# Reordering the input loads, the constants' queue and the first statistics of a macaron block on one Trainium2 core

## The chip, the cores and the metric

The kernel runs on 1 core of one Trainium2 chip. The metric is the device time in microseconds (us) of one execution. A core has TensorE (PE, with its weight loads PEld), VectorE (DVE), ScalarE (ACT), GpSimd (POOL) and SyncE (SP), which only issues DMAs here. All DMAs of a core share 16 DMA engines.

## The reference, cut to what matters

Four sequences of 512 tokens with 512 features go through half a feed-forward network, a Mamba-2 mixer and half a feed-forward network again, each with a layer norm in front and a residual behind. The weights of the feed-forward network are seen through a Walsh-Hadamard transform (fwht), random signs and scales:

```python
def ffn(x):                                   # INTER = 2048, SCALE = 64
    x = fwht(x * SU_ug) / SCALE
    up   = x @ W_up.T   * (Wscale_ug[:INTER] * SCALE)
    gate = x @ W_gate.T * (Wscale_ug[INTER:] * SCALE)
    x = fwht(silu(gate) * up * SU_dp) / SCALE
    return x @ W_down.T * (Wscale_dp * SCALE)

x = x + 0.5 * ffn(layernorm(x))
x = x + mixer(layernorm(x))
x = x + 0.5 * ffn(layernorm(x))
```

The change touches only what stands ahead of and in the first pieces of the first feed-forward network.

## The kernel before

`program` lays out the memory and calls `begin` (the first feed-forward network for two sequences, and the preparation of all weights) and `mixer` (everything after). Only `begin` is changed. Each engine has its own program in it (`@block.sync`, `gpsimd`, `tensor`, `scalar`, `vector`), and runs it strictly in the order written; semaphores tie the five together.

**Transforming the weights.** The Hadamard transform is folded into the weights. The down weights `wdn` come in FB = 16 *groups* of 256 KB. A group i is loaded by SP into `group_tile(i)` (parts of `res`, `draw`, `mraw`, `last`, L346), multiplied on PE by the small Hadamard matrix `H16` (L464, bank 4 + i % 4), copied out of the bank by ACT (L588), scaled by `wdp`, and stored by SP into the HBM buffer `mid_s` ("down_half" in the trace, L367). Who scales depends on i: POOL for i < 4 (L434), VectorE straight out of the bank for even i of 8 and above (L711), and VectorE after ACT's copy for the others (L714). The later stage of the down weights reads two 128-row blocks of `mid_s` at a time (`fetch_down`, L308), and SP waits for all 16 stores before the first of them.

The up and gate weights come in NC = 8 chunks of 1 MB in `raw` (`fetch`, L300). Four elementwise operations, the *butterflies* (VectorE at L785 and L788 for chunk 0, POOL at L412 and L416 for the others), and then one *turn* for each of KH = 4 blocks transform them: a PE matmul with the Hadamard matrix H (L492), a high part rounded by ACT (L600) and a low part made by VectorE (L726), both into `wu`. `keep_up` stores `wu` to HBM (2 MB) for the later network (L312).

**x.** A tile of 128 tokens is loaded into `res` (x of sequence 0 by L351, of sequence 1 by L352, of both others by L375), VectorE takes its statistics (`bn_stats`, L792) and computes the inverse root in some 20 tiny dependent operations (`roots`, with `rsqrt`, L162 to L139), `bias` (L741) finishes it and raises `s_mv`, ACT normalizes the rows (`rows`, L614), PE transposes them (`turn(("x", c, t))`, four 128 x 128 transposes, L484), ACT makes the high part (L596) and VectorE the low part (L722). The roots of both sequences are computed together, for 8 tiles at once.

**Order.** PE does groups 0 to 3, the 4 turns of chunk 0 ("ug", 0, k), groups 4 to 7, the 4 turns of sequence 0 ("x", 0, t), groups 8 and 9. Then *units* follow, n = 0 to 15: unit n is chunk n // 2 of the weights for sequence n % 2. A unit has four `up(n, j)` of 12 matmuls (L508), and between them what `unit_turns(n)` says; in unit 0 also groups 10 to 15. `turns` numbers the turns in order of execution; the number picks the PSUM bank (`turn_bank`: `U[i % 4]` for the first eight, then two banks `T`), and for i of 10 and above PE waits for the low part of turn i - 2 (`s_tl`). At the end of unit 1 stands `down(0)`, and the first turn of the down weights ("dn", 0, 0) (L495) is in unit 1 behind `up(1, 1)`; it needs `fetch_down(0)`.

SP's queue before: the four constant loads (`cs` twice, `pr`, `wdp`, all on `s_par`), `fetch(0)`, groups 0 to 3, x of sequence 0, x of sequence 1, then a wait for x of sequence 0 to have landed (`s_x0`), groups 4 to 11, `fetch(1)`, groups 12 to 15, the scales `sc`, and then the 16 stores in order, with `fetch(2)` behind the store of group 4 and `keep_up(0)` behind that of group 8.

Of the kernel before, what the change touches and what calls it, by code (L numbers as in the profile page):

```python
# [57 lines left out]
def run(steps):  # L58
    for _ in steps:
        pass  # L60
# [110 lines left out]
def begin(nc, s, x, wug, wsc, wdn, win, wout, cst, par, ug_s, dn_s, in_s, out_s, mid_s):  # L171
# [6 lines left out]
    turns = {}  # L178
    for key in ([("ug", 0, k) for k in range(KH)] + [("x", 0, t) for t in range(TPG)] + [("x", 1, t) for t in range(TPG)]
                + [("ug", 1, 0), ("dn", 0, 0), ("ug", 1, 1), ("dn", 0, 1), ("ug", 1, 2), ("ug", 1, 3)]):  # L180
        turns[key] = len(turns)
# [12 lines left out]
    with ExitStack() as ctx:  # L194
# [17 lines left out]
        st, mv = sb("st", [P, 2 * TPG, 6]), sb("mv", [P, 4, 2 * TPG])  # L212
        s_par, s_c, s_ex, s_x0, s_x1, s_x, s_sc = (sem(n) for n in "par c ex x0 x1 x sc".split())
        s_g, s_gv, s_gc, s_gp, s_gw, s_gs = (sem(n) for n in "g gv gc gp gw gs".split())
# [20 lines left out]
        def by_vector(i):  # L235

            return i >= 8 and i % 2 == 0

# [27 lines left out]
        def unit_turns(n):  # L266

            c, g = n // 2, n % 2
            if n == 0:
                return (), (("x", 1, 0), ("x", 1, 1)), (("x", 1, 2), ("x", 1, 3)), ()  # L270
            if n == 1:
                return (), (("ug", 1, 0), ("dn", 0, 0)), (("ug", 1, 1), ("dn", 0, 1)), (("ug", 1, 2), ("ug", 1, 3))
            if n == UNITS - 2:
                return (("dn", c, 0),), (("dn", c, 1),), (("x", 2, 0), ("x", 2, 1)), (("x", 2, 2), ("x", 2, 3))
            if n == UNITS - 1:
                return (), (), (), ()
            return (("dn", c, g),), (("ug", c + 1, 2 * g),), (("ug", c + 1, 2 * g + 1),), ()
# [15 lines left out]
        def _(sp):  # L293
# [46 lines left out]
            xt = x.rearrange("(t p) n -> p t n", p=P)  # L340
            sp.dma_start(cs[:, 0:C_I2], cst[:, 0:C_I2]).then_inc(s_par, 16)
            sp.dma_start(cs[:, C_I2:C_END], cst[:, 5 * P:5 * P + HEADS]).then_inc(s_par, 16)
            sp.dma_start(pr[:], par[:, 0:P_WDP]).then_inc(s_par, 16)
            sp.dma_start(wdp[:], par[:, P_WDP:P_END]).then_inc(s_par, 16)
            def load_group(i):
                sp.dma_start(group_tile(i), wdn[PQ * i:PQ * (i + 1)].rearrange("i (a n) -> a i n", a=FB)).then_inc(s_gl[i], 16)  # L346

            fetch(0)
            for i in range(4):
                load_group(i)  # L350
            sp.dma_start(res[:, 0:TPG, :], xt[:, 0:TPG, :]).then_inc(s_x0, 16)  # L351
            sp.dma_start(res[:, TPG:2 * TPG, :], xt[:, TPG:2 * TPG, :]).then_inc(s_x1, 16)  # L352
            sp.wait_ge(s_x0, 16)
            for i in range(4, 12):
                load_group(i)
            fetch(1)
            for i in range(12, FB):
                load_group(i)
            sp.dma_start(sc[:], wsc.rearrange("c p n -> p c n")).then_inc(s_sc, 16)
            for i in range(FB):  # L360
                if i < 4:
                    sp.wait_ge(s_gp, i + 1)
                elif by_vector(i):
                    sp.wait_ge(s_gv, scaled_before(i) + 1)
                else:
                    sp.wait_ge(s_gw, copies(i) - 3)
                sp.dma_start(mid_s[:, PQ * i:PQ * (i + 1), :], group_tile(i)).then_inc(s_gs, 16)  # L367
                if i == 4:
                    fetch(2)
                if i == 8:  # L370
                    keep_up(0)
            sp.wait_ge(s_gs, 16 * FB)
            fetch_down(0)
            fetch_down(1)
            sp.dma_start(res[:, 2 * TPG:NT, :], xt[:, 2 * TPG:NT, :]).then_inc(s_x, 16)  # L375
            fetch(3)
            keep_down(0)
            fetch_down(2)
            keep_up(1)
            for c in range(1, NC):  # L380
# [24 lines left out]
        def _(pool):  # L405
# [24 lines left out]

            pool.wait_ge(s_par, 64)
            for i in range(4):
                pool.wait_ge(s_gc, i + 1)
                pool.tensor_tensor(group_tile(i), group_tile(i), wdp[:], ALU.mult).then_inc(s_gp, 1)  # L434
            pool.wait_ge(s_gw, FB // 2)
            butterflies(1, False)
# [14 lines left out]
        def _(pe):  # L451
# [100 lines left out]

            pe.wait_ge(s_par, 64)
            pe.wait_ge(s_c, 8)
            for i in range(4):
                group(i)
            for k in range(KH):
                turn(("ug", 0, k))
            for i in range(4, 8):
                group(i)  # L560
            for t in range(TPG):
                turn(("x", 0, t))
            group(8)
            group(9)
            for n in range(UNITS):
# [19 lines left out]
        def _(act):  # L585
# [21 lines left out]
            def rows(c, ts=range(TPG)):  # L607

                act.wait_ge(s_mv, max(1, c))
                if c:  # L610
                    act.wait_ge(s_tm, turns["x", c - 1, TPG - 1] + 1)
                for t in ts:
                    at = TPG * (0, 1, 1, 0)[c] + t
                    act.activation(xn[:, t, :], res[:, TPG * (0, 1, 2, 0)[c] + t, :], ACT.Identity,  # L614
                                   bias=mv[:, 1, at:at + 1], scale=mv[:, 3, at:at + 1]).then_inc(s_row, 1)
# [30 lines left out]

            act.wait_ge(s_par, 64)
            act.activation(s["acol"][:], pr[:, P_ALOG:P_ALOG + 1], ACT.Exp).then_inc(s_ex, 1)
            act.wait_ge(s_c, 8)
            for i in range(4):  # L650
                group(i)
            for k in range(KH):
                turn(("ug", 0, k))
            group(4)
            group(5)
            rows(0)
            for t in range(TPG):
                turn(("x", 0, t))
            group(6)
            group(7)  # L660
            group(9)
            rows(1)
            act.wait_ge(s_sc, 16)
# [6 lines left out]
            for n in range(UNITS - 1):  # L670
                keys = unit_turns(n)
                silu(n, 0)
                if n == 0:
                    group(11)
                    group(13)
                for key in keys[0]:
                    turn(key)
                silu(n, 1)
                if n == 0:
                    group(15)  # L680
                for key in keys[1]:
                    turn(key)
                if n == UNITS - 2:
                    rows(2)
                for key in keys[2]:
                    turn(key)
                for j in range(2):
                    hidden_high(n, j)
                for key in keys[3]:
                    turn(key)  # L690
                high_blocks(n)
                for key in halves_of(n + 1):
                    high_half(key)
# [11 lines left out]
        def _(dve):  # L705
# [64 lines left out]
            dve.memset(s["ones"][:], 1.0).then_inc(s_c, 1)  # L770
            dve.wait_ge(s_par, 64)
            dve.tensor_reduce(eight[:], I.rearrange("p (a i) -> p i a", i=PQ), mybir.AxisListType.X, ALU.add).then_inc(s_c, 1)
# [8 lines left out]
            dve.wait_ge(s_ex, 1)  # L781
            dve.tensor_scalar(s["acol"][:], s["acol"][:], -1.0, None, ALU.mult).then_inc(s_c, 1)
            dve.wait_ge(s_fr[0], 16)
            for n, op in enumerate((ALU.add, ALU.subtract)):
                dve.tensor_tensor(t1[:, n::2, :], raw[:, 0, 0::2, :], raw[:, 0, 1::2, :], op).then_inc(s_b0, 1)  # L785
            dve.wait_ge(s_b0, 2)
            for n, op in enumerate((ALU.add, ALU.subtract)):
                dve.tensor_tensor(raw[:, 0, 2 * n:2 * n + 2, :], t1[:, 0:2, :], t1[:, 2:4, :], op).then_inc(s_b0, 1)  # L788
            for landed, c in ((s_x0, 0), (s_x1, 1)):
                dve.wait_ge(landed, 16)  # L790
                for t in range(TPG * c, TPG * c + TPG):
                    own.done(dve.bn_stats(st[:, t, :], res[:, t, :]))  # L792
            run(roots(dve, st, mv, own))
            bias(0, 2 * TPG)
            for k in range(KH):
                turn(("ug", 0, k))
            for t in range(TPG):
                turn(("x", 0, t))
            for i in (8, 4, 5, 6, 7, 9):
                group(i)  # L800
            def low_blocks(n):
# [6 lines left out]
            for n in range(UNITS - 1):  # L808
                keys = unit_turns(n)
                if n == 0:  # L810
                    for i in range(10, 14):
                        group(i)
                for key in keys[0]:
                    turn(key)
                if n == 0:
                    group(14)
                    group(15)
                for key in keys[1]:
                    turn(key)
                if n == 0:  # L820
                    for key in keys[2]:
                        turn(key)
                hidden(n, 0)
                if n:
                    for key in keys[2]:
                        turn(key)
                hidden(n, 1)
# [1358 lines left out]
```

## Time and profile before

| | |
|---|---|
| median of 3 runs | 1654.56 us (1654.16 to 1661.31) |
| profiled execution, its own time | 1658.09 us |
| its span | 1656.2 us |
| PE busy | 1621.9 us, 98% of the span |
| VectorE, ScalarE, GpSimd busy | 1033.3, 626.5 and 377.0 us |
| first matmul starts | 11.37 us |
| first `up` starts | 32.64 us |
| second unit's first `up` starts | 51.39 us |
| DMA in the first 60 us | 17.44 MB, 291 GB/s |

The profile is one execution; its span is 1.9 us shorter than that execution's own time. The timeline names engine, line, output and input tile, and behind an entry in brackets, how long the engine had been idle and what released it. "xN" merges N instructions of one kind. A matmul of f32 is recorded as two entries.

### The profile page before, as it was taken

What the parts mean: (1) busy time and instruction counts of PE and PEld (TensorE: products, weight loads), DVE (VectorE), ACT (ScalarE), POOL (GpSimd) and SP (SyncE); (2) the same over time, 40 slices, a digit from 0 to 9 for tenths busy, and PEclk for the clock granted to TensorE, in tenths of its full rate; (3) what the DMA queues carried; (4) which work ended last, traced back from release to release, by engine and by line L of the source; (5) the groups of instructions that cost most, each with busy time, mean ns of one, the idle gap of its engine ahead of it and who ended that gap; (6) DMA issues with size and microseconds to landing.
All of it is one profiled execution on the core that took longest, in us unless ns stands there. A gap on an engine that the chain in (4) does not pass through costs nothing.

```text
span 1656.2 us, 25046 instructions
## 1 busy us (share of the span) xinstructions
PE 1621.9 (98%) x9672; PEld 1311.9 (79%) x9672; DVE 1033.3 (62%) x2022; ACT 626.5 (38%) x934; POOL 377.0 (23%) x298
## 2 busy tenths in 40 slices
PE   6999999989999999999999999999999999999999
PEld 3788788867888778888877888877888877888887
DVE  6444345766676877777786677777675683543333
ACT  4334334454333464333355334256333341122111
POOL 1655662012222212222122122122122121000000
PEclk9999999999999999999999999999999999999999
DMA  9755654744455354444435445545544447556763
GB/s 286 293 190 208 224 196 165 254 167 157 155 157 167 130 176 148 158 161 151 163 119 174 165 150 166 162 135 184 165 155 156 155 128 217 166 178 187 219 199 131
DMA packets 253427, 290.46 MB, mean 175 GB/s; under 512 B 14464, under 2 KB 211200, under 8 KB 244096
## 3 DMA queue, kind: packets, MB, share of 16 engines
q1 hardware_dynamic: 253312, 288.88, 53.4%
q8 instruction: 78, 1.28, 0.3%
q14 instruction: 37, 0.30, 0.1%
HBM read 238.51 MB, written 50.33 MB: 174 GB/s over the span
## 4 chain that ended last, share of the span: by engine, by line
PE 72%; DVE 4%; ACT 2%; issue 1%; DMA 0%; SPq 0%; ACTq 0%; DVEq 0%
PE bank L1184 30%; PE bank L1225 14%; PE bank L1140 12%; PE bank L1253 5%; PE bank L1322 3%; PE bank L1293 2%; PE bank L1309 2%; PE bank L1271 2%; PE bank L1316 1%; PE bank L1281 1%; DVE xT L1740 0%; DVE m_cv L1781 0%; DVE res L1766 0%; PE bank L1168 0%; PE bank L1150 0%
## 5 line engine op out<-in xcount | busy, mean ns | idle before, releaser
L1184 PE MATMUL bank<-fxT,wj 128*128 128x512 f32 x1752 | 415.3, 390 | 1.2 <-DVE xn L1753 1.2
L1184 PEld LDWEIGHTS bank<-fxT,wj 128*128 128x128 f32 x1752 | 328.7, 188 | 70.1 <-DVE xn L1753 1.7
L1225 PE MATMUL bank<-m_wd,m_hb 128*128 128x512 f32 x1128 | 278.8, 393 | 1.9 <-DVE m_hb L1759 1.9
L1225 PEld LDWEIGHTS bank<-m_wd,m_hb 128*128 128x128 f32 x1128 | 209.1, 188 | 47.3 <-issue 5.0
L1535 ACT CAST m_hb<-xn 128x512 fp32r<-128x512 f32 x96 | 59.5, 620 | 455.1 <-DVE xn L1753 455.1
L1140 PE MATMUL bank<-xT,wi 128*128 128x512 f32 x900 | 222.6, 395 | 1.6 <-DVE m_cv L1781 0.5
L1140 PEld LDWEIGHTS bank<-xT,wi 128*128 128x128 f32 x900 | 166.1, 188 | 39.1 <-issue 4.5
L1766 DVE TENSOR_TENSOR res<-bank,res 128x512 f32<-128x512 f32 x192 | 132.5, 690 | 83.4 <-PE bank L1225 81.2
L2084 POOL TENSOR_TENSOR m_L<-m_L,m_GT 128x512 f32<-128x512 f32 x36 | 52.6, 1461 | 436.0 <-ACT m_L L1544 436.0
L1753 DVE SCALAR_TENSOR_TENSOR xn<-bank,sc,xn 128x512 f32<-128x512 f32 x96 | 71.8, 748 | 123.0 <-PE bank L1184 122.9
L1529 ACT ACTIVATE xn<-bank,sc 128x512 f32<-128x512 f32 x96 | 66.1, 688 | 145.8 <-PE bank L1184 140.3
L1544 ACT ACTIVATE m_L<-bank 128x512 f32<-128x512 f32 x128 | 76.5, 598 | 84.1 <-PE bank L1271 83.8
L1759 DVE TENSOR_TENSOR m_hb<-xn,m_hb 128x512 fp32r<-128x512 f32 x96 | 66.3, 691 | 56.0 <-ACT m_hb L1535 56.0
L1781 DVE SCALAR_TENSOR_TENSOR m_cv<-bank,pr,m_cv 128x511 f32<-128x511 f32 (+2 forms) x120 | 89.6, 747 | 11.4 <-ACT m_cv L1489 8.6
L508 PE MATMUL bank<-xT,b_wu 128*128 128x512 f32 x384 | 95.5, 397 | 0.0
L508 PE MATMUL bank<-b_xT,b_wu 128*128 128x512 f32 x384 | 93.0, 392 | 0.0
L1253 PE MATMUL bank<-m_wo,m_yh 128*128 128x512 f32 x384 | 90.8, 391 | 0.7 <-ACT xn L1529 0.7
L549 PE MATMUL bank<-b_wd,b_hb 128*128 128x512 f32 x384 | 90.9, 392 | 0.0
L2111 POOL TENSOR_TENSOR m_ss<-m_ss,m_y 128x512 f32<-128x512 f32 x28 | 36.2, 1293 | 239.6 <-ACT m_y L1564 239.6
L508 PEld LDWEIGHTS bank<-xT,b_wu 128*128 128x128 f32 x384 | 71.8, 188 | 17.9 <-DVE xT L722 0.5
L1253 PEld LDWEIGHTS bank<-m_wo,m_yh 128*128 128x128 f32 x384 | 71.6, 188 | 17.7 <-issue 1.9
L508 PEld LDWEIGHTS bank<-b_xT,b_wu 128*128 128x128 f32 x384 | 72.1, 188 | 16.3 <-issue 0.7
(222 smaller groups left out, 2312.4 us busy)
## 6 DMA issues: line engine op xcount, KB each, us to landing
wj<-ug_split SPq DMA_DIRECT2D x167, 512.0 KB, 4.2
m_wd<-dn_split SPq DMA_DIRECT2D x48, 1024.0 KB, 4.8
wi<-in_split SPq DMA_DIRECT2D x76, 512.0 KB, 3.3
ug_split<-b_wu SPq DMA_DIRECT2D x8, 2048.0 KB, 14.1
m_wo<-out_split SPq DMA_DIRECT2D x32, 512.0 KB, 4.1
wi<-ug_split SPq DMA_DIRECT2D x25, 512.0 KB, 4.1
in_split<-b_msp SPq DMA_DIRECT2D x20, 512.0 KB, 3.7
raw<-in_wug SPq DMA_DIRECT2D x8, 1024.0 KB, 7.0
```

The costliest lines, as they stand in the source:

```text
L508: ins = pe.matmul(U[j][:], wu[c % 2][:, a, k, ck(j)], xT[g][:, b, k, :], start=(k == 0 and i == 0), stop=(k == KH - 1 and i == 2))
L549: ins = pe.matmul(down_bank(n, t)[:], hb[:, n % 2, a, j, ck(t)], wd[c % 2][:, b, j, :], start=(j == 0 and i == 0), stop=(j == 1 and i == 2))
L1140: ins = pe.matmul(to[:], w[:, a, k, :], xT[:, b, k, :], start=(k == 0 and i == 0), stop=(k == KH - 1 and i == 2))
L1184: ins = pe.matmul(to[:], w[:, a, k, :], frm[:, b, k, :], start=(k == 0 and i == 0), stop=(k == KH - 1 and i == 2))
L1225: ins = pe.matmul(F[t % 2][:], hb[:, a, j, ck(t)], wd[:, b, j, :], start=(j == 0 and n == 0), stop=(j == 1 and n == 2))
L1253: ins = pe.matmul(F[1 - t % 2][:], yh[:, (2 * pair + i) % 4, a, ck(t)], wout[i][:, b, :], start=(i == 0 and n == 0), stop=(i == 1 and n == 2))
L1529: act.activation(hf[:, j, :], F[1][:], ACT.Silu, scale=sc[:, at % NC, j:j + 1]).then_inc(s_sil, 1)
L1544: act.activation(L[:, b % 2, j, :], A[:], ACT.Exp).then_inc(s_L, 1)
L1753: dve.scalar_tensor_tensor(hf[:, j, :], F[0][:], sc[:, at % NC, 2 + j:3 + j], hf[:, j, :], ALU.mult, ALU.mult).then_inc(s_h, 1)
L1759: dve.tensor_tensor(hb[:, 1, j, :], hf[:, j, :], hb[:, 0, j, :].bitcast(F32), ALU.subtract).then_inc(s_lo, 1)
L1766: dve.tensor_tensor(r, frm[:], r, ALU.add).then_inc(s_acc, 1)
L1781: ins = dve.scalar_tensor_tensor(cv[:, d:SEQ], frm[:, 0:SEQ - d], pr[:, w + 3 - d:w + 4 - d], cv[:, d:SEQ], ALU.mult, ALU.add)
```

## The change

- SP's queue: x of sequence 0 is the first load, then groups 0 to 3, `fetch(0)`, groups 4 to 7, x of sequence 1, groups 8 to 15, `fetch(1)`; the wait for x of sequence 0 is gone. `fetch(2)` moves to just ahead of the store of group 15, and `keep_up(0)` behind `fetch_down(1)`. A wait on `s_us` stands ahead of `keep_up(1)`.
- The constants and `sc` are issued by ScalarE. `wdp` gets a semaphore of its own, `s_wdp`, so what needs only `cs` and `pr` no longer waits for it.
- POOL scales groups 0 to 7 (before: 0 to 3), VectorE 8 to 15. The predicate `by_vector` gives the same answers as before.
- PE and ScalarE: behind groups 0 to 3 come the turns of x of sequence 0, groups 4 and 5, the turns of chunk 0, and groups 6 to 9 (ACT: 6, 7 and 9).
- VectorE: the statistics and roots of sequence 0 alone come first, ahead of the butterflies of chunk 0; those of sequence 1 are done between groups 9 and 12, in three pieces around groups 10 and 11.
- Unit 0: all four turns of sequence 1 come behind `up(0, 2)` (before: two behind `up(0, 1)`, two behind `up(0, 2)`). ACT's `rows(1)` comes behind its copy of group 15; VectorE does `hidden(0, 0)` ahead of those turns' low parts.

```diff
-    for key in ([("ug", 0, k) for k in range(KH)] + [("x", 0, t) for t in range(TPG)] + [("x", 1, t) for t in range(TPG)]
+    for key in ([("x", 0, t) for t in range(TPG)] + [("ug", 0, k) for k in range(KH)] + [("x", 1, t) for t in range(TPG)]
...
-                return (), (("x", 1, 0), ("x", 1, 1)), (("x", 1, 2), ("x", 1, 3)), ()
+                return (), (), tuple(("x", 1, t) for t in range(TPG)), ()
...
@@ SP
-            fetch(0)
+            sp.dma_start(res[:, 0:TPG, :], xt[:, 0:TPG, :]).then_inc(s_x0, 16)
             for i in range(4):
                 load_group(i)
-            sp.dma_start(res[:, 0:TPG, :], xt[:, 0:TPG, :]).then_inc(s_x0, 16)
+            fetch(0)
+            for i in range(4, 8):
+                load_group(i)
             sp.dma_start(res[:, TPG:2 * TPG, :], xt[:, TPG:2 * TPG, :]).then_inc(s_x1, 16)
-            sp.wait_ge(s_x0, 16)
-            for i in range(4, 12):
+            for i in range(8, FB):
                 load_group(i)
             fetch(1)
-            for i in range(12, FB):
-                load_group(i)
-            sp.dma_start(sc[:], wsc.rearrange("c p n -> p c n")).then_inc(s_sc, 16)
             for i in range(FB):
-                if i < 4:
+                if i == FB - 1:
+                    fetch(2)
+                if i < FB // 2:
                     sp.wait_ge(s_gp, i + 1)
...
-                    sp.wait_ge(s_gw, copies(i) - 3)
+                    sp.wait_ge(s_gw, copies(i) - FB // 2 + 1)
                 sp.dma_start(mid_s[:, PQ * i:PQ * (i + 1), :], group_tile(i)).then_inc(s_gs, 16)
-                if i == 4:
-                    fetch(2)
-                if i == 8:
-                    keep_up(0)
             sp.wait_ge(s_gs, 16 * FB)
             fetch_down(0)
             fetch_down(1)
+            keep_up(0)
...
+            sp.wait_ge(s_us, 16)
             keep_up(1)
@@ POOL
-            pool.wait_ge(s_par, 64)
-            for i in range(4):
+            pool.wait_ge(s_wdp, 16)
+            for i in range(FB // 2):
...
-            pool.wait_ge(s_gw, FB // 2)
+            pool.wait_ge(s_gw, FB // 4)
@@ PE
-            pe.wait_ge(s_par, 64)
+            pe.wait_ge(s_par, 48)
...
+            for t in range(TPG):
+                turn(("x", 0, t))
+            group(4)
+            group(5)
             for k in range(KH):
                 turn(("ug", 0, k))
-            for i in range(4, 8):
+            for i in range(6, 10):
                 group(i)
-            for t in range(TPG):
-                turn(("x", 0, t))
-            group(8)
-            group(9)
@@ ACT
+            act.dma_start(cs[:, 0:C_I2], cst[:, 0:C_I2]).then_inc(s_par, 16)
+            act.dma_start(pr[:], par[:, 0:P_WDP]).then_inc(s_par, 16)
+            act.dma_start(cs[:, C_I2:C_END], cst[:, 5 * P:5 * P + HEADS]).then_inc(s_par, 16)
+            act.dma_start(wdp[:], par[:, P_WDP:P_END]).then_inc(s_wdp, 16)
+            act.dma_start(sc[:], wsc.rearrange("c p n -> p c n")).then_inc(s_sc, 16)
+            act.wait_ge(s_par, 48)
...
-            for k in range(KH):
-                turn(("ug", 0, k))
-            group(4)
-            group(5)
             rows(0)
             for t in range(TPG):
                 turn(("x", 0, t))
+            group(4)
+            group(5)
+            for k in range(KH):
+                turn(("ug", 0, k))
             group(6)
             group(7)
             group(9)
-            rows(1)
...
                 if n == 0:
                     group(15)
+                    rows(1)
@@ VectorE
+            dve.wait_ge(s_x0, 16)
+            for t in range(TPG):
+                own.done(dve.bn_stats(st[:, t, :], res[:, t, :]))
+            run(roots(dve, st[:, 0:TPG], mv[:, :, 0:TPG], own))
+            bias(0, TPG)
             dve.wait_ge(s_fr[0], 16)
...
-            for landed, c in ((s_x0, 0), (s_x1, 1)):
-                dve.wait_ge(landed, 16)
-                for t in range(TPG * c, TPG * c + TPG):
-                    own.done(dve.bn_stats(st[:, t, :], res[:, t, :]))
-            run(roots(dve, st, mv, own))
-            bias(0, 2 * TPG)
+            for t in range(TPG):
+                turn(("x", 0, t))
             for k in range(KH):
                 turn(("ug", 0, k))
-            for t in range(TPG):
-                turn(("x", 0, t))
-            for i in (8, 4, 5, 6, 7, 9):
-                group(i)
+            dve.wait_ge(s_wdp, 16)
+            group(8)
+            group(9)
+            second = stats(TPG, TPG, TPG)
+            dve.wait_ge(s_x1, 16)
+            next(second)
+            next(second)
+            group(10)
+            group(11)
+            next(second)
+            bias(TPG, TPG)
```

## Rows read from the trace of the kernel before

**Rows 1.** Busy time by stage: stretch, its us, each engine, granted clock, DMA share, GB/s.

```profile
0.00:11.37 11.37, 0.00 (x1) 0.04 (x1) 2.32 (x9) 1.49 (x2) 0.20 (x4) 1.00 0.82 232
11.37:32.64 21.27, 17.64 (x44) 8.55 (x44) 17.46 (x44) 12.09 (x20) 5.72 (x4) 0.92 0.98 286
32.64:60.00 27.36, 25.90 (x106) 18.23 (x105) 15.57 (x21) 13.18 (x21) 14.63 (x6) 1.00 0.88 318
60.00:470.00 410.00, 401.24 (x2089) 325.16 (x2088) 226.10 (x409) 168.87 (x266) 154.27 (x109) 1.00 0.56 194
...
27.60:31.10 3.50, 3.47 (x17) 3.33 (x18) 2.67 (x5) 3.43 (x6) 0.00 (x0) 0.53 1.01 327
```

**Rows 2.** PE's timeline, 11 to 57 us.

```profile
11.37 5.07 PE L464 MATMUL bank<-res,b_H 128*128 128x512 f32 x8 [11.37 <-DMA res<-in_wdn]
16.27 3.60 PE L492 MATMUL bank<-raw,cs 128*128 128x512 f32 x8
20.83 4.13 PE L464 MATMUL bank<-res,b_H 128*128 128x512 f32 x8 [0.97 <-DMA res<-in_wdn]
27.63 3.50 PE L484 MATMUL bank<-cs,xn 128*128 128x128 f32 x16 [2.67 <-ACT xn L614]
30.92 2.04 PE L464 MATMUL bank<-draw,b_H 128*128 128x512 f32 x4
32.64 3.13 PE L508 MATMUL bank<-xT,b_wu 128*128 128x512 f32 x12
...
44.01 1.09 PE L484 MATMUL bank<-cs,xn 128*128 128x128 f32 x8 [0.29 <-DVE last L711]
...
51.39 5.66 PE L508 MATMUL bank<-b_xT,b_wu 128*128 128x512 f32 x24
```

**Rows 3.** Durations (ns min/median/max) of the matmuls of the first groups.

```profile
L464 PE MATMUL bank<-res,b_H x8: 592/625/1192, 11.4 to 15.8; 128*128 128x512 f32 x8
```

**Rows 4.** ScalarE's timeline, 13 to 30 us.

```profile
13.51 0.59 ACT L588 COPY res<-bank 128x512 f32<-128x512 f32 x1 [8.32 <-PE bank L464]
...
26.67 2.93 ACT L614 ACTIVATE xn<-res,b_mv 128x512 f32<-128x512 f32 x4 [3.09 <-DVE b_mv L741]
```

**Rows 5.** VectorE's timeline, 4 to 33 us.

```profile
4.99 0.38 DVE L772 TENSOR_REDUCE b_eight<-cs 128x8 f32<-128x128 f32 x1 [3.99 <-DMA b_wdp<-in_par]
...
12.79 2.36 DVE L788 TENSOR_TENSOR raw<-b_t 128x1024 f32<-128x1024 f32 x2
16.65 2.47 DVE L792 BATCH_NORM_STATS2 b_st<-res 128x6 f32<-128x512 f32 x4 [1.50 <-DMA res<-in_x]
19.88 2.48 DVE L792 BATCH_NORM_STATS2 b_st<-res 128x6 f32<-128x512 f32 x4 [0.76 <-DMA res<-in_x]
...
26.47 0.17 DVE L741 SCALAR_TENSOR_TENSOR b_mv<-b_mv 128x8 f32<-128x8 f32 x1
...
30.10 2.49 DVE L722 TENSOR_TENSOR xT<-bank,xT 128x512 fp32r<-128x512 f32 x4 [0.83 <-ACT xT L596]
```

**Rows 6.** POOL's timeline, 14 to 56 us.

```profile
14.24 5.72 POOL L434 TENSOR_TENSOR res<-res,b_wdp 128x512 f32<-128x512 f32 x4 [13.80 <-ACT res L588]
45.15 4.74 POOL L412 TENSOR_TENSOR b_t<-raw 128x1024 f32<-128x1024 f32 x2 [25.19 <-DVE last L714]
49.97 5.29 POOL L416 TENSOR_TENSOR raw<-b_t 128x1024 f32<-128x1024 f32 x2
```

**Rows 7.** Durations, as in rows 3, of POOL's scaling and of VectorE's low parts.

```profile
L434 POOL TENSOR_TENSOR res<-res,b_wdp x4: 1262/1266/2034, 14.2 to 18.7; 128x512 f32<-128x512 f32 x4
...
L753 DVE TENSOR_TENSOR b_hb<-b_hf,b_hb x32: 679/687/2715, 52.3 to 329.3; 128x512 fp32r<-128x512 f32 x32
```

**Rows 8.** DMA issues, 0 to 60 us: count, KB each, median us to landing.

```profile
draw<-down_half SPq DMA_DIRECT2D x2, 512.0 KB, 4.1
...
down_half<-last SPq DMA_DIRECT2D x2, 256.0 KB, 6.2
```

**Rows 9.** What PE waited for, 0 to 62 us: total, times, longest.

```profile
PE bank L495 <- DMA draw<-down_half: 1.2, 1, 1.2
```

More of the change, by code:

```diff
@@ L212, in begin @@
         st, mv = sb("st", [P, 2 * TPG, 6]), sb("mv", [P, 4, 2 * TPG])
-        s_par, s_c, s_ex, s_x0, s_x1, s_x, s_sc = (sem(n) for n in "par c ex x0 x1 x sc".split())
+        s_par, s_wdp, s_c, s_ex, s_x0, s_x1, s_x, s_sc = (sem(n) for n in "par wdp c ex x0 x1 x sc".split())
         s_g, s_gv, s_gc, s_gp, s_gw, s_gs = (sem(n) for n in "g gv gc gp gw gs".split())
@@ L235, in by_vector @@
         def by_vector(i):
-            return i >= 8 and i % 2 == 0
+            return i >= FB // 2 and i % 2 == 0
         def copies(i):
@@ L340, in _ @@
             xt = x.rearrange("(t p) n -> p t n", p=P)
[L341 to L344, printed above, removed]
             def load_group(i):
                 sp.dma_start(group_tile(i), wdn[PQ * i:PQ * (i + 1)].rearrange("i (a n) -> a i n", a=FB)).then_inc(s_gl[i], 16)
-            fetch(0)
+            sp.dma_start(res[:, 0:TPG, :], xt[:, 0:TPG, :]).then_inc(s_x0, 16)
             for i in range(4):
                 load_group(i)
-            sp.dma_start(res[:, 0:TPG, :], xt[:, 0:TPG, :]).then_inc(s_x0, 16)
+            fetch(0)
+            for i in range(4, 8):
+                load_group(i)
             sp.dma_start(res[:, TPG:2 * TPG, :], xt[:, TPG:2 * TPG, :]).then_inc(s_x1, 16)
-            sp.wait_ge(s_x0, 16)
-            for i in range(4, 12):
+            for i in range(8, FB):
                 load_group(i)
             fetch(1)
-            for i in range(12, FB):
-                load_group(i)
-            sp.dma_start(sc[:], wsc.rearrange("c p n -> p c n")).then_inc(s_sc, 16)
             for i in range(FB):
-                if i < 4:
+                if i == FB - 1:
+                    fetch(2)
+                if i < FB // 2:
                     sp.wait_ge(s_gp, i + 1)
@@ L607, in rows @@
             def rows(c, ts=range(TPG)):
-                act.wait_ge(s_mv, max(1, c))
+                act.wait_ge(s_mv, c + 1)
                 if c:
@@ L645, in high_half @@
                 act.copy(parts[:, halves[key][1], 0, :], untransformed(key)).then_inc(s_ph, 1)
-            act.wait_ge(s_par, 64)
+            act.dma_start(cs[:, 0:C_I2], cst[:, 0:C_I2]).then_inc(s_par, 16)
[4 more added lines that the diff above has]
+            act.wait_ge(s_par, 48)
             act.activation(s["acol"][:], pr[:, P_ALOG:P_ALOG + 1], ACT.Exp).then_inc(s_ex, 1)
@@ L770, in _ @@
             dve.memset(s["ones"][:], 1.0).then_inc(s_c, 1)
-            dve.wait_ge(s_par, 64)
+            dve.wait_ge(s_par, 48)
             dve.tensor_reduce(eight[:], I.rearrange("p (a i) -> p i a", i=PQ), mybir.AxisListType.X, ALU.add).then_inc(s_c, 1)
@@ L810, in _ @@
                 if n == 0:
-                    for i in range(10, 14):
+                    for i in range(12, FB):
                         group(i)
@@ L814, in _ @@
                     turn(key)
-                if n == 0:
-                    group(14)
-                    group(15)
                 for key in keys[1]:
                     turn(key)
-                if n == 0:
-                    for key in keys[2]:
-                        turn(key)
                 hidden(n, 0)
-                if n:
-                    for key in keys[2]:
-                        turn(key)
+                for key in keys[2]:
+                    turn(key)
                 hidden(n, 1)
```

## The prediction, made before the changed kernel was run

> **What bounds the kernel now.** I read the busy time by stage first, because the change touches only the start. After 60 us PE is busy 401.24 of 410.00 us [rows 1]: the kernel is PE-bound there, and nothing the change edits runs later than the first units. So what it can give or take is the time at which PE is done with its early work, and that shift then goes through to the end. Next I read PE's own timeline. PE does nothing for 11.37 us, until group 0 has landed [rows 2]; from there to the first `up` at 32.64 it is busy 17.64 of 21.27 us [rows 1]. The idle pieces are 0.97 us (group 4 has not landed) and 2.67 us (the rows of sequence 0 are not normalized) [rows 2]. Behind 32.64 the only waits are 0.29 us [rows 2] and 1.2 us for the first down weights coming back from HBM [rows 9]. The whole prize is small: 11.37 us of start, some 5 us up to 32.64, 1.5 us after it. Times below are those of the profiled execution, whose own time is 3.5 us above the median; I carry the differences over to the median of 1654.56.
>
> **What is late in the start.** VectorE's timeline: x of sequence 0 lands at 16.65, that of sequence 1 at 19.88, the roots of both together run from the end of the statistics, 22.36, to 26.64 (4.3 us of tiny dependent steps) [rows 5], and ACT starts its rows at 26.67 [rows 4]. The DMA engines are full (shares of 0.82, 0.98 and 0.88) [rows 1], so order alone decides when each input arrives.
>
> **The first matmul.** Before, the constants (476 KB), chunk 0 (1 MB) and group 0 (256 KB) are ahead of it. Now it is the constants on another queue, x of sequence 0 (1 MB) and group 0: the same bytes at the same 232 GB/s [rows 1]. Saved are four issues of SP ahead of the first large load; lost is what `sc` takes, and that constants and x interleave. I take group 0 at 11.0 us instead of 11.37; the bounds are 1.5 us to either side, a little more than one 256 KB group at 232 GB/s (1.1 us). The Trainium skill (DMA: Bandwidth & Descriptors, section Issuing engines are not separate DMA queues) says that DMAs of different issuing engines interleave on the same 16 DMA engines and that a second issuer saves only issue time; by that rule the start stays at 11.4, as in my sum within 0.4 us. The constants were used at 4.99 and H16 was ready 1.3 us later [rows 5]; even 4 us later they would not be last ahead of group 0.
>
> **Step 1: groups 0 to 3.** They took 16.27 - 11.37 = 4.9 us [rows 2], with first matmuls of 1192 ns against a least of 592 ns [rows 3]. Unchanged: from 11.0 to 15.9.
>
> **Step 2: rows and turns of sequence 0.** The roots no longer wait for sequence 1 and come ahead of the butterflies. x lands after the first 1.5 MB instead of after 3.6 MB (16.65): at 232 GB/s plus the first 2 us some 8.5 us. Statistics 2.47 and roots 4.3 [rows 5] give 15.3. ACT's copy of group 3 ends 0.27 + 0.59 behind PE, as for group 0 [rows 4], at 16.75, later than the roots: so the 2.67 us wait for the roots is gone, and a new one replaces it. PE is through with group 3 and has nothing behind it but the transposes (before: the turns of chunk 0). The first row takes 0.8 us, so PE idles from 15.9 to 17.55; four rows at the 2.93 us of before [rows 4] pace the transposes to about 20.2. Groups 4 and 5 are there now, since SP no longer waits for x (group 4 landed 4.2 us after x did, 20.83 against 16.65 [rows 2, 5]), and take 0.86 each, as groups 8 and 9 in 30.92 to 32.64 [rows 2]: 21.8.
>
> **Step 3: the turns of chunk 0.** They need the butterflies and, for the banks, the low part of x's first tile. Chunk 0 now lands where x did, behind 3.6 MB, a little ahead of 16.65 [rows 5], say 16.4. Four butterflies are 4.8 us (2.36 for two [rows 5]), to 21.2, and a low part 0.62 [rows 5], to 21.9: just in time for PE, if nothing slows them. But POOL scales groups 0 to 3 from about 13.9 to 19.0 at 1.27 us each. The trace shows what the two do to each other: POOL's scaling took 2034 ns once against a median of 1266, the one begun at 14.24 while VectorE's butterfly of 12.79 to 15.15 ran [rows 5 to 7], and VectorE's low part took 2715 ns once against 687 [rows 7] under POOL's butterflies of 49.97 [rows 6]. Before, POOL's other scalings ran beside statistics, which have one SBUF input, and were not slowed. Now two or three lie in the way of the butterflies. Alternating with them costs VectorE up to two POOL operations, 2.5 us; the least is nothing, if chunk 0 lands behind POOL's last. I take 2.5, since at 16.4 two of POOL's four are still to come. The butterflies end at 23.7, and the turns start at 24.4.
>
> This is also what the Trainium skill says (SBUF — State Buffer, section SBUF: two separate sides): a VectorE instruction with both inputs in SBUF and a GpSimd one that reads SBUF exclude each other, and the second waits for the whole of the first. The trace agrees (2034 and 2715 ns); without that rule and those rows the step would cost nothing.
>
> **Step 4: to the first up.** Four turns at 0.86 (3.44, of the 3.60 with its tail [rows 2]) and groups 6 to 9, again 3.44: 31.3, or 28.8 without the interference. Before: 32.64. Gain 1.3, or 3.8. VectorE's low parts of chunk 0 end 1 to 2 us ahead of that, and the loads of groups 8 and 9 lie within the first 6.5 MB, at 286 GB/s [rows 1] 25 us.
>
> **Step 5: unit 0.** It took 51.39 - 32.64 = 18.75 us [rows 2], 0.29 of it a wait that goes. The four turns of sequence 1 now stand together. There are two banks; the third turn waits until the first one's low part is done, ACT is in its rows until shortly after `up(0, 2)` ends, and VectorE does `hidden(0, 0)` ahead of it. By the durations (ACT 0.55, VectorE 0.65, two transposes' 1.09 [rows 2]) PE stands about 1.1 us; bounds 0.5 and 2. Net a loss of 0.8: the gain is 0.5 here, or 3.0.
>
> **Step 6: the down weights.** The first turn of the down weights waited 1.2 us [rows 9]. Now 2 MB (`keep_up(0)`) stand behind `fetch_down` instead of ahead of the last stores. Group 15 is scaled at about 41.7, its store behind `fetch(2)` lands 6.2 us after issue [rows 8], near 48.5, and the weights 4.1 us later [rows 8], 52.6; PE wants them near 56. The wait goes: +1.2. Butterflies of chunk 1 on POOL start where group 15 is scaled and take 10.1 us [rows 6]: 51.9, needed at 55. Moving SP's other loads (`fetch(2)`, x of sequences 2 and 3) is hidden: they are used past 52 us. POOL's four more scalings end near 30, and only stores wait for them.
>
> **Step 7: the clock.** TensorE's granted clock was 0.53 of full speed, nearly all at 1.2 instead of 2.4 GHz, in 27.6 to 31.1 us [rows 1], right behind the 2.67 us idle, where the transposes had to wait for ACT anyway. In the new order PE idles 1.65 us and then, with the interference, 2.6 us ahead of eight dense turns and groups. A stretch like that at half clock there costs up to 1.7 us; the least is nothing. I take 0.8.
>
> **Sum.** 1.3 - 0.8 + 1.2 - 0.8 = 0.9 us gained with the interference, 3.4 without. Forecast 1654.56 - 0.9, rounded to 1653.5 us. A difference of less than 0.5% (8.3 us) counts as no change, about what a measurement of this kernel can tell.
>
> **Rivals.**
> - *The head is rid of its waits* (0.33): chunk 0 lands behind POOL's last scaling, or VectorE wins each turn. Then 3.4 to 4.2 us, and up to 1.5 more if group 0 lands early: 1649 to 1651.5. For it: no queue waits for x any more. Against: the overlap of two scalings.
> - *The down weights come late, and it is slower* (0.05). All 16 groups now go in ahead of chunk 1 and their stores behind it. 14.1 MB have to pass ahead of the last store's end; at 318 GB/s [rows 1] that is 46 us. At the 232 GB/s of the head it is 63, the weights are there at 67, and PE, which wants them at 56, stands 11 us: some 9 us slower, 1664. It decides from a last store later than 52 us. Against it: that rate was never so low between 11 and 60 us.
> - *The start comes later* (0.10): x's small rows and `sc` hold up group 0 by 1.5 us, and the clock takes its 1.7: 1656 to 1657.5.
> - *My forecast* (0.52): interference and the new waits eat most; 1652 to 1656.
>
> **How the numbers follow.** The likeliest case gives 1653.5. The range takes in the second case from its low end and the fourth: 1649 to 1657.5; outside stay the slower rival and the ends of the others. Faster by over 0.5% would need half of the idle time before 60 us to vanish, start included: 0.03. Slower by over 0.5% is the down weights and what I overlook: 0.05. The rest, 0.92, is no change.
>
> **What would show it.** PE's timeline after: first matmul near 11.0 (else step 1 is wrong); an idle of 1.65 us ahead of L484 released by ACT's rows; the turns of chunk 0 (L492) near 24.4 with VectorE's butterflies over 1.22 us each, or near 22 without; the first `up` near 31.3; an idle near 1 us among sequence 1's transposes; no wait at L495; the granted clock in the stretch behind each idle. Wrong it would be if group 0 landed much earlier than 11 us, so that bytes in front of it are not what counts, or if a stretch later than 60 us changed its idle time.

## The result and the profile after

The changed kernel is slower: 1661.63 us, the median of 6 runs (1659.59 to 1664.77), against 1655.17 us (1654.03 to 1661.31). The ratio is 1.0029, 95% interval 1.0019 to 1.0040. That is within the 0.5% that I called no change, but on the other side of it than forecast, and outside the range. Timed again over 10 runs, the same kernel gave 1.0030 (1.0020 to 1.0040; e5 below).

PE's timeline, with what answers to [rows 2]:

```profile
10.92 6.30 PE L458 MATMUL bank<-res,b_H 128*128 128x512 f32 x8 [10.92 <-DVE acol L781]
22.44 3.67 PE L478 MATMUL bank<-cs,xn 128*128 128x128 f32 x16 [5.21 <-ACT xn L608]
25.90 2.16 PE L458 MATMUL bank<-res,b_H 128*128 128x512 f32 x4
27.90 3.60 PE L486 MATMUL bank<-raw,cs 128*128 128x512 f32 x8
...
34.37 3.36 PE L502 MATMUL bank<-xT,b_wu 128*128 128x512 f32 x12
...
50.36 1.25 PE L478 MATMUL bank<-cs,xn 128*128 128x128 f32 x8 [1.03 <-DVE b_xT L721]
...
54.24 5.61 PE L502 MATMUL bank<-b_xT,b_wu 128*128 128x512 f32 x24
```

The wait for the rows of sequence 0 did not go, it doubled: 5.21 us instead of 2.67. The first `up` starts at 34.37 (before 32.64). The first matmul is released by VectorE's set-up, that is by the constants, no longer by group 0. Why the rows are late stands in VectorE's timeline:

```profile
9.61 0.38 DVE L771 TENSOR_REDUCE b_eight<-cs 128x8 f32<-128x128 f32 x1 [8.61 <-DMA cs<-in_cst]
...
10.74 2.46 DVE L784 BATCH_NORM_STATS2 b_st<-res 128x6 f32<-128x512 f32 x4
13.23 0.17 DVE L162 TENSOR_TENSOR b_mv<-b_st 128x4 f32<-128x4 f32 x1
...
13.85 1.23 DVE L167 SCALAR_TENSOR_TENSOR b_mv<-b_mv 128x4 f32<-128x4 f32 x1
...
15.53 1.14 DVE L131 TENSOR_SCALAR b_mv<-b_mv 128x4 f32<-128x4 f32 x1
...
17.10 1.25 DVE L138 TENSOR_TENSOR b_mv<-b_mv 128x4 f32<-128x4 f32 x1
18.38 1.19 DVE L139 SCALAR_TENSOR_TENSOR b_mv<-b_mv 128x4 f32<-128x4 f32 x1
...
21.37 0.16 DVE L740 SCALAR_TENSOR_TENSOR b_mv<-b_mv 128x4 f32<-128x4 f32 x1
21.45 2.35 DVE L789 TENSOR_TENSOR b_t<-raw 128x1024 f32<-128x1024 f32 x2
```

and in POOL's:

```profile
13.80 1.27 POOL L428 TENSOR_TENSOR res<-res,b_wdp 128x512 f32<-128x512 f32 x1 [13.36 <-ACT res L582]
15.37 1.26 POOL L428 TENSOR_TENSOR res<-res,b_wdp 128x512 f32<-128x512 f32 x1 [0.31 <-ACT res L582]
17.07 2.48 POOL L428 TENSOR_TENSOR res<-res,b_wdp 128x512 f32<-128x512 f32 x2 [0.43 <-ACT res L582]
```

Four root steps take 1.14 to 1.25 us instead of 0.17; each starts just behind the start of a scaling of POOL and ends within 0.04 us of its end. The roots take 8.3 us (13.23 to 21.53), before 4.3 [rows 5]. The butterflies come behind the last scaling and run at full speed (2.35 us for two, before 2.36).

The DMA issues of the first 60 us show the constants' way (KB, median us from issue to landing); the same loads took 1.9 to 2.8 us before, `sc` 10.1:

```profile
b_wdp<-in_par ACTq DMA_DIRECT2D x1, 256.0 KB, 9.4
cs<-in_cst ACTq DMA_DIRECT2D x1, 128.0 KB, 3.7
pr<-in_par ACTq DMA_DIRECT2D x1, 44.0 KB, 6.6
cs<-in_cst ACTq DMA_DIRECT2D x1, 32.0 KB, 7.9
sc<-in_wsc ACTq DMA_DIRECT2D x1, 16.0 KB, 17.3
```

Aligned on the residual adds, which both kernels do in the same order, and counted from each trace's first matmul, the changed kernel is 1.8 us behind at the first add and 1.8 us behind at the 62nd, 325 us in; at the 65th, 381 us in, it is 5.1 us behind, and 5.4 us at the last. Nothing of the change runs there. The busy time by stage, columns as in rows 1, of the changed kernel:

```profile
21.00:24.40 3.40, 1.96 (x9) 1.97 (x10) 3.30 (x6) 2.83 (x4) 0.00 (x0) 0.50 1.06 274
24.40:26.50 2.10, 2.10 (x10) 1.84 (x9) 2.10 (x3) 1.88 (x5) 0.00 (x0) 0.51 1.05 265
...
366.00:377.50 11.50, 8.64 (x24) 5.93 (x26) 5.75 (x10) 5.37 (x9) 0.00 (x0) 0.58 0.21 78
```

and of the kernel before, the late stretch:

```profile
366.00:377.50 11.50, 9.30 (x107) 7.09 (x107) 8.69 (x20) 6.81 (x10) 1.28 (x1) 1.00 0.44 150
```

In the changed kernel's execution most of that stretch, from 367.8 us on, ran at 1.2 GHz. It is the mixer's beginning, where PE waits 0.56, 1.64 and 0.69 us in either kernel.

### The profile page after: what moved, and what is told of

It is laid out like the page before. It is cut to its first block, busy times and chain, and to the rows that moved or that the text cites. A ratio compares the mean times of both kernels' runs of the same rounds, so it can differ in the third digit from the quotient of the medians.

```text
span 1661.2 us, 25072 instructions
## 1 busy us (share of the span) xinstructions
PE 1626.0 (98%) x9672; PEld 1315.7 (79%) x9672; DVE 1039.3 (63%) x2041; ACT 626.6 (38%) x934; POOL 381.0 (23%) x302
## 4 chain that ended last, share of the span: by engine, by line
PE 72%; DVE 4%; ACT 2%; issue 1%; DMA 0%; SPq 0%; ACTq 0%; DVEq 0%
PE bank L1184 30%; PE bank L1225 14%; PE bank L1140 12%; PE bank L1253 5%; PE bank L1322 3%; PE bank L1293 2%; PE bank L1309 2%; PE bank L1271 2%; PE bank L1316 1%; PE bank L1281 1%; DVE xT L1740 0%; DVE m_cv L1781 0%; DVE res L1766 0%; PE bank L1168 0%; PE bank L1150 0%
```

## The experiments

Each was timed beside the kernel before, and each ratio is to those runs. Times differ by a microsecond or two between such sets, so kernels of different sets are compared by their ratios. Of each I read PE's timeline:

| | ratio (95%) | first matmul | idle ahead of sequence 0's transposes | first up, behind first matmul |
|---|---|---|---|---|
| before, trace above | | 11.37 | 2.67 | 21.27 |
| changed, trace above | 1.0029 (1.0019 to 1.0040) | 10.92 | 5.21 | 23.45 |
| e1 before again | 0.9997 (0.9986 to 1.0008) | 9.56 | 2.85 | 21.62 |
| e5 changed again | 1.0030 (1.0020 to 1.0040) | 11.11 | 5.05 | 23.62 |
| e2 POOL held back | 0.9984 (0.9974 to 0.9995) | 9.92 | 1.78 | 18.35 |
| e3 constants on SP | 1.0024 (1.0013 to 1.0036) | 10.13 | 4.31 | 23.23 |
| e4 both | 0.9990 (0.9979 to 1.0000) | 10.86 | 1.39 | 18.37 |
| e8 before, POOL on the roots | 1.0017 (1.0008 to 1.0025) | 9.39 | 4.79 | 23.97 |
| e6 before, keep_up late | 1.0005 (0.9996 to 1.0013) | 9.40 | 2.35 | 21.18 |
| e7 e4, groups 4 and 5 ahead | 0.9997 (0.9988 to 1.0006) | 11.48 | 0.73, ahead of group 4 | 18.64 |
| e11 e7, two groups before x | 1.0015 (1.0006 to 1.0025) | 6.70 | 2.29, ahead of group 4 | 23.58 |
| e9 changed, filled | 1.0025 (1.0016 to 1.0034) | 11.06 | 5.64 | 22.90 |
| e10 e7, filled | 1.0002 (0.9993 to 1.0011) | 12.34 | 2.34, ahead of group 4 | 19.14 |

**e1, the kernel before again.**

> The kernel before, unchanged, to see its own scatter and a second trace of it. In the changed kernel's trace the shift against before was 1.4 us at 70 us and 1.3 us at 340 us, and then grew to 5 us behind a stretch at half granted clock near 367 us. Theory A (that stretch is chance, and any kernel with this mixer can fall into it): some of these runs have a mean clock near 0.995 and are 3.5 to 4 us longer than the others with 0.998 or 0.999; the ratio is 1.000. Theory B (only the changed kernel falls into it): all runs have 0.998 or 0.999 and lie within 2 us.

Of its 12 runs three have a mean clock of 0.996 and take 1658.0 to 1660.0 us, so the kernel before loses time to the clock too, as theory A has it, though by less than the 3.5 to 4 us that it names. The runs with 0.998 go up to 1659.15 as well, so the clock is not all of the scatter. The traced run itself has no late stretch at half clock; those of e6 and e8, which are the kernel before with one edit at the start, do. Its first matmul is at 9.56, in e6 and e8 at 9.4; the 11.37 that I predicted from was a late one. It cost less than it looks: groups 0 to 3 then took 5.07 us, in e1 6.59, and ended at 16.4 and 16.2.

**e2, POOL held back.**

```diff
             pool.wait_ge(s_wdp, 16)
+            pool.wait_ge(s_b0, 4)
```

> The changed kernel, with POOL's scaling held back until VectorE's roots of sequence 0 and its butterflies are done. Theory POOL (GpSimd's scalings of 13.8 to 19.5 us stretch VectorE's tiny root steps from 4.2 to 8.2 us): the roots take 4.2 us again, the rows start near 17.9 instead of 21.57, the first up starts near 30.6 to 31.5 instead of 34.37, and the kernel is 2.5 to 3.8 us faster than the changed one. Theory constants (what is late is only the start of the statistics at 10.74): the roots stay at 8 us and the first up stays within 0.5 us of 34.4. If all of the change's loss came from the clock, neither moves the end.

ScalarE's timeline shows the rows directly behind the last copy, released by roots that take 4.1 us again:

```profile
15.54 0.58 ACT L583 COPY res<-bank 128x512 f32<-128x512 f32 x1 [0.27 <-PE bank L459]
16.41 2.94 ACT L609 ACTIVATE xn<-res,b_mv 128x512 f32<-128x512 f32 x4 [0.28 <-DVE b_mv L741]
```

The first `up` starts at 28.27, 5.1 us earlier against the first matmul than in the changed kernel: 3.4 us are the idle time, 1.0 us is that PE did not fall to half clock (the transposes took 2.78 us instead of 3.67), and 0.7 us is that groups 0 to 3 took 5.59 us instead of 6.30, which differs from one execution to the next (e5: 6.47). With 1654.80 us this is the fastest version measured, 0.9984 of the kernel before. The theory POOL holds, and the gain is larger than the 2.5 to 3.8 us expected: from 1.0030 (e5) to 0.9984 is some 7.5 us. The traces show 6.1 us of it at the first `up` (34.37 to 28.27); 1.0 us of that is an earlier first matmul, which the edit does not explain.

**e3, the constants first on SP's queue.**

```diff
+            sp.dma_start(cs[:, 0:C_I2], cst[:, 0:C_I2]).then_inc(s_par, 16)
+            sp.dma_start(pr[:], par[:, 0:P_WDP]).then_inc(s_par, 16)
+            sp.dma_start(cs[:, C_I2:C_END], cst[:, 5 * P:5 * P + HEADS]).then_inc(s_par, 16)
             sp.dma_start(res[:, 0:TPG, :], xt[:, 0:TPG, :]).then_inc(s_x0, 16)
...
-            act.dma_start(cs[:, 0:C_I2], cst[:, 0:C_I2]).then_inc(s_par, 16)
-            act.dma_start(pr[:], par[:, 0:P_WDP]).then_inc(s_par, 16)
-            act.dma_start(cs[:, C_I2:C_END], cst[:, 5 * P:5 * P + HEADS]).then_inc(s_par, 16)
```

> The changed kernel, with the three small constant loads back on SP's queue ahead of x; wdp and sc stay on ScalarE's. Theory constants (they share the DMA engines with x and the groups and so landed at 9.6 instead of 5.0): VectorE's set-up runs near 5, the statistics start when x lands, 8 to 9 us, the first matmul at 9.5 to 10.9, and the roots end 1.5 to 2.5 us earlier than 21.4, part of it because fewer root steps meet POOL; 1 to 2 us faster than the changed kernel. Theory POOL alone: the roots still meet all of POOL's scalings and the first up moves by less than 0.7 us.

VectorE's set-up starts at 5.00 instead of 9.61 and the statistics at 9.30 instead of 10.74, but the roots meet POOL still: they take 8.2 us and end at 19.99. PE's first matmul now waits for group 0, at 10.13. The first `up` is 1.0 us earlier in the trace, 0.2 us against the first matmul. 1.0024 against 1.0030 can't be told apart, so this part is worth under a microsecond or two; the expected 1 to 2 us is not shown.

**e4, both.**

> Both edits of the last two together. If the two causes are separate their gains add: roots end near 15.3, the rows start when ACT has copied group 3 (near 17), the first up starts at 29 to 30.5, and the kernel is 4 to 5 us faster than the changed one and 1 to 3 us faster than the kernel before. If they are one and the same delay, it is no faster than the better of the two alone.

The first `up` is at 29.23 and the kernel no better than e2. The roots end at 16.41, as in e2 (16.38), since x landed at 9.75 only; ACT starts the rows at 17.57, behind the copy of group 3. The gains do not add.

**e5, the changed kernel again.**

> The changed kernel itself again, beside the next three. Theory structure: 1.003 times the kernel before, 3 to 6 us; the first up starts 23.3 to 23.6 us behind the first matmul (before: 21.3 and 21.6 in two traces), and the statistics wait for the constants at 8.5 to 9.7 us. Theory chance (its loss was the runs that it happened to get): a ratio of 1.001 or less.

Structure, not chance: 1.0030 again. The first `up` is 23.62 us behind the first matmul, the roots take 8.3 us with the same four steps held (1.13 to 1.26 us), and the constants come at 9.79.

**e8, the damage done to the kernel before.**

```diff
             pool.wait_ge(s_par, 64)
+            pool.wait_ge(s_x1, 16)
             for i in range(4):
```

> The kernel before, with one wait added: POOL starts its four scalings when x of sequence 1 has landed (19.8 us) instead of at 14.2, so that they run beside the roots of 22.4 to 26.6. Nothing else moves: the stores of groups 0 to 3 are issued behind 25 us anyway. Theory POOL: several root steps take 1.1 to 1.25 us instead of 0.17, the roots take 6 to 8 us instead of 4.3, the wait for the rows grows from 2.7 to 4.5 to 6 us, and the kernel is 2 to 4 us slower than before. Rival (the roots of the changed kernel were long for another reason, the smaller tiles or the DMA load): they stay at 4.3 us and the time is the same.

VectorE's timeline has the roots of both sequences meeting the rest of POOL's scalings (17.96 to 22.92):

```profile
20.36 0.17 DVE L162 TENSOR_TENSOR b_mv<-b_st 128x8 f32<-128x8 f32 x1
20.45 1.26 DVE L163 TENSOR_TENSOR b_mv<-b_st 128x8 f32<-128x8 f32 x1
21.63 0.16 DVE L164 TENSOR_TENSOR b_mv<-b_st 128x8 f32<-128x8 f32 x1
21.83 1.13 DVE L165 TENSOR_SCALAR b_mv<-b_mv 128x8 f32<-128x8 f32 x1
22.87 0.15 DVE L166 SCALAR_TENSOR_TENSOR b_mv<-b_mv 128x8 f32<-128x8 f32 x1
```

Two steps are hit, the roots take 6.3 us, the wait for the rows is 4.79, and the kernel is 1.0017 times as long (2.6 us by the medians, 2 to 4 expected). With e2 this shows the cause from both sides.

**e6, `keep_up(0)` late in the kernel before.**

```diff
-                if i == 8:
-                    keep_up(0)
...
             fetch_down(1)
+            keep_up(0)
...
+            sp.wait_ge(s_us, 16)
             keep_up(1)
```

> The kernel before, with keep_up(0) moved behind fetch_down(1) alone (and the wait ahead of keep_up(1) that this needs). Theory: the 2 MB store is what made the last group stores land late; the 1.2 us wait ahead of the first turn of the down weights goes, and the kernel is 1.0 to 1.2 us faster. Rival: the stores are late because group 15 is scaled late; then the wait stays and the time is the same.

The wait for the down weights is gone, and no gain can be measured. In e1, the kernel before itself, and in e8 PE has no idle time there either. So e6 can't tell the two theories apart, and the 1.2 us of [rows 9] belong to that one execution; why its weights came late is not shown.

**e7, groups 4 and 5 ahead of the transposes.** On top of e4:

```diff
-            for i in range(4):
+            for i in range(6):
                 group(i)
             for t in range(TPG):
                 turn(("x", 0, t))
-            group(4)
-            group(5)
```

and on ScalarE the two copies stand directly behind `rows(0)`.

> The changed kernel with both repairs (POOL behind the butterflies, constants first on SP), and groups 4 and 5 ahead of the turns of sequence 0 on PE and their copies behind the rows on ScalarE. Theory order: PE's 1.4 to 1.8 us idle ahead of the transposes is filled with two groups, the first up starts 1.0 to 1.7 us earlier against the first matmul than the 18.4 us with both repairs alone. Rival (the groups have not landed by then, or the chain over ScalarE and VectorE is what sets the first up): within 0.5 us of 18.4, and the time is the same as with both repairs.

The rival holds (18.64 us, and 0.9997 against e4's 0.9990, with intervals that overlap). The idle time moves: PE now waits 0.93 us ahead of chunk 0's turns, for the low part of x, which stands on VectorE behind the butterflies, and these began when chunk 0 had landed:

```profile
17.76 2.36 DVE L788 TENSOR_TENSOR b_t<-raw 128x1024 f32<-128x1024 f32 x2 [0.61 <-DMA raw<-in_wug]
```

**e11, two groups ahead of x.** On top of e7, `load_group(0)` and `load_group(1)` stand ahead of x in SP's queue.

> The kernel of e7 with groups 0 and 1 loaded ahead of x of sequence 0. The first matmul starts at 6.5 to 8 us instead of 10 to 11. Theory x bounds (statistics, roots and rows of sequence 0 set the first up): x lands 1 to 2 us later and the first up starts 1 to 2 us later, the kernel is that much slower than e7 in spite of the earlier first matmul. Theory first matmul bounds: the first up starts 1 to 3 us earlier.

The first matmul starts at 6.70, 4.8 us earlier than in e7, and the first `up` at 30.28, 0.2 us later; the kernel is slower than e7, by 1659.74 to 1656.61 us. An early first matmul buys nothing here. The theory that x bounds is right in kind, but the 1 to 2 us later `up` that it names did not come. PE's timeline shows it working in pieces:

```profile
6.70 3.75 PE L464 MATMUL bank<-res,b_H 128*128 128x512 f32 x4 [6.70 <-DVE acol L782]
12.63 2.40 PE L464 MATMUL bank<-res,b_H 128*128 128x512 f32 x4 [2.18 <-DMA res<-in_wdn]
17.32 3.74 PE L464 MATMUL bank<-res,b_H 128*128 128x512 f32 x4 [2.29 <-DMA res<-in_wdn]
```

The first `up` alone doesn't explain 3 us; mean clocks of 0.995 to 0.997 in seven of its 11 runs (e7: one) may be part of it. The granted clock was at half from 14.1 to 20.9 us, behind the first of these idle pieces.

**e9 and e10, PE kept busy at the mixer's beginning.** Two matmuls whose result nobody reads, in the 1.6 us wait:

```diff
+                if j == 0 and q == 0 and b == 0:
+                    for _ in range(2):
+                        pe.matmul(S[1][:], I, xc[:, 0, :], start=True, stop=True)
```

> The changed kernel plus two matmuls of 128x512 that compute nothing needed, written to a bank that is free there, in the 1.6 us gap ahead of the first decay matmul of the mixer (near 367 us). Theory clock by gap (granted clock falls to half because TensorE is thinly used in that stretch of 7 us): no run has the late half-clock stretch, the mean clocks stay at 0.997 to 0.999 and the runs with 0.994 or 0.995 are gone; the median is 0 to 2 us below the changed kernel's. Theory clock by chance (unrelated to that gap): as many runs at 0.995 or less as in the changed kernel, and the median 0 to 1.7 us above it.

> The kernel of e7 with the two idle matmuls ahead of the mixer's first decay matmul, as in e9. If the late half-clock stretch is one of thin use of TensorE, no run has a mean clock under 0.998, the scatter shrinks to 3 us, and the median is 0.5 to 2 us below that of e7, 3 to 5 us below the kernel before. Otherwise the scatter is that of e7 and the median up to 1.7 us above it.

In neither trace is the late stretch at half clock. The busy time from 360 to 380 us, columns as in rows 1, of e6, e7 and e10:

```profile
360.00:380.00 20.00, 16.81 (x135) 12.16 (x134) 11.85 (x27) 9.26 (x14) 1.27 (x1) 0.74 0.35 112
360.00:380.00 20.00, 16.03 (x148) 11.99 (x145) 13.59 (x29) 10.04 (x15) 1.28 (x1) 0.91 0.35 113
360.00:380.00 20.00, 17.66 (x181) 12.99 (x180) 14.83 (x31) 10.04 (x15) 1.29 (x1) 1.00 0.37 116
```

All 13 traces, with the time from the 62nd residual add to the last:

| granted clock, 360 to 380 us | traces | 62nd to last add |
|---|---|---|
| 1.00 | before, e1, and the filled e9 and e10 | 1318.9, 1319.2, 1319.8, 1319.5 |
| 0.91 | e3, e4, e7, e11 | 1320.1, 1320.1, 1319.9, 1321.0 |
| 0.83 | e5, e8 | 1322.2, 1321.8 |
| 0.74 | changed, e2, e6 | 1322.5, 1321.6, 1323.7 |

So nine of the 11 traces without the two matmuls have the late stretch, also those of e2, the fastest version, and of e6, the kernel before with one edit. It costs from about 1 us to almost 5 us, and it is not peculiar to the changed kernel. Neither filled trace has it. The mean clocks agree: none below 0.997 in e9's 10 runs (e5: three of 10 at 0.995 or 0.996), and 1.000 in eight of e10's 11 runs (e7: one of 11). PE busy through that wait is what kept the clock up, as far as these runs go. The median went from 1662.09 to 1660.40 in e9, but in e10 it did not fall (1657.20, e7 1656.61), and the kernel is not the expected 3 to 5 us below the one before (1.0002). In e7's trace the late stretch cost little, so there was little to win back. e10's scatter is 4.4 us all the same: its runs differ by something else, which I did not find.

## Why the prediction was wrong

- **Step 1** said that constants 4 us later would not be last ahead of group 0. They came 4.6 us later (9.61 against 4.99 [rows 5]) and were last, ahead of the first matmul and of the statistics. The time, 10.92, looks like the 11.0 predicted, but 11.37 was a late start of the kernel before; that the number fits is luck. Against the three other traces with the old order of loads (e1, e6 and e8, 9.4 to 9.6) the first matmul is about 1.4 us later. The constants alone do not explain it: with them early, group 0 itself lands at 10.1 to 12.3, behind x (e3, e4, e7, e10). Groups 0 to 3 took 6.3 us instead of the 4.9 I kept: the first six matmuls took 1.05 to 1.19 us each, where in the trace I predicted from only three did. That trace was the short one; e1 has 6.6 us. A slip without weight: the constants ahead of group 0 were 460 KB, 476 counts `sc` too.
- **Step 2 is the step that failed.** "Statistics 2.47 and roots 4.3 give 15.3": measured 21.53. The statistics began 2.2 us later, and the roots took 8.3 us. I had the rule and its rows in step 3, and applied it only to the large operations; for the roots beside POOL's scalings I put the cost at nothing, without a reason. The timeline shows POOL's next scaling starting in the gap between two tiny steps, and the step behind it taking as long as that scaling lasts, 1.14 to 1.25 us. PE idled 5.21 us instead of 1.65. e2, which takes POOL away, has the roots at 4.1 us and the idle time at 1.78.
- **Step 3**: the butterflies were not touched, because the roots had already held them back until POOL was done (21.45, POOL's last scaling ends at 19.55). The 2.6 us that I charged there fell away.
- **Step 4**: the first `up` at 34.37, predicted 31.3. By parts: groups 0 to 3 ended 1.3 us later than predicted, the idle time was 3.6 longer, transposes and groups 4 and 5 took 5.46 us instead of 4.25, the butterflies cost 2.6 less, the rest 0.4 less: +3.1.
- **Step 5 was right**: 1.03 us of waiting among the transposes, and unit 0 took 19.87 us against 18.75, +1.1 for the +0.8 predicted.
- **Step 6**: the wait for the down weights went, as predicted, but the 1.2 us booked as a gain were no fixed cost: e1 and e8, with the old order, do not have them.
- **Step 7** was right in kind, and too small. Granted clock was 0.50 from 21.0 to 26.5, behind the 5.21 us idle; e2, e4 and e7, whose idle pieces are 1.8 us and less, have none there. In between it is not settled: with pieces of 2.2 to 2.4 us the clock fell in e11 and did not in e6 and e10. I had not looked at what the clock does elsewhere: the stretch near 367 us cost 3.3 us in this trace. The Trainium skill (TensorE: Matmul & The Clock Gate, section HAM oscillation) warns of idle gaps behind which the clock falls. The early stretch agrees (5.21 us idle); the late one came with no idle piece over 1.64 us from 360 us on, in work of small matmuls.

Of the 5.0 us between the two spans, 1.8 are the start counted from the first matmul, less 0.45 for a first matmul 0.45 earlier in these two traces, 3.3 the late stretch, and some 0.3 later differences. Two traces of each kernel say more about the start. The first residual add, behind nearly all that the change touches, comes at 72.28 and 72.99 us in the changed kernel and at 70.88 and 68.04 in the kernel before: 1.4 to 5.0 us later, 3.2 in the mean, of a difference of 5 between the medians. In e2 it comes at 66.20. Whether the changed kernel falls into the late stretch more often or for longer is open. Both of its traces have it and neither of the kernel before has, but e6 and e8 have it too. The mean clock is 0.995 or less in 4 of its 16 runs and 0.996 or less in 3 of e1's 12, with a start that itself differs in clock.

## What to carry to other kernels

A chain of tiny dependent VectorE operations on SBUF is exposed beside a GpSimd stream that reads SBUF: here a step of 0.17 us took as long as the GpSimd operation of 1.27 us beside it, four times in one chain. Look whether GpSimd's work can wait until the chain is through (one wait took this kernel from 1.0030 to 0.9984). Small loads that gate everything did not become early by a queue of their own (9.61 us); ahead of the large ones they were there at 5.0, though here group 0 and x then came last, and no time was won that could be measured. Before a wait or a late start is booked as a gain, see it in a second trace of the kernel before.

## What the runs showed that I had not expected

The step L131 (a `tensor_scalar` of one SBUF input, 128x4) was held too, 1.14 us (1.26 in e3), and L165 in e8, 1.13 us. The Trainium skill (SBUF — State Buffer, section SBUF: two separate sides) has such an instruction contend only in VectorE's two-port modes; the trace doesn't show modes, so that these were in one is a guess. ScalarE's five loads, 476 KB in all, took up to 9.4 us (`wdp`) and 17.3 us (`sc`) beside SP's large ones, against 2.8 us for `wdp` when it stood ahead of the large ones, and 10.1 us for `sc` behind them, on SP's one queue. In all 13 traces the first three to seven matmuls took 0.8 to 1.2 us, most of them 1.06, against the later 0.59, while the granted clock reads 1.00 there: the clock column alone does not show this slow beginning.
